# Where the weight casts are issued, and which queue loads the cast weights, in an attention and mixture-of-experts layer on eight cores

## The reference

```
q, k, v = heads(xn @ Wq.T), heads(xn @ Wk.T), heads(xn @ Wv.T)      # 32 heads of 64
z = q @ k.T / 8
lom = where(j < i, -softplus(z), 0);  s = reversed cumsum(lom) - lom
att = where(j < i, exp(log_sigmoid(z) + s), 0)
a = concat(att @ v) @ Wo.T
we = top-4 of softmax(xn @ gate.T), normalized                      # 32 experts
rg, ru = xn @ Rg.T, xn @ Ru.T                                       # 2048 -> 128
y = sum_e we[e] * (((silu(rg @ Ug[e].T @ Cg[e].T) * (ru @ Uu[e].T @ Cu[e].T)) @ Rd.T) @ Ud[e].T @ Cd[e].T)
sh = the same form with a shared expert of width 2816
out = x + a + y + sh
```

## Time and profile before

| | us |
|---|---|
| median of 3 runs | 8175.34 |
| fastest and slowest of them | 8138.22, 8181.30 |
| the profiled execution, its own time | 8143.93 |
| its span on the slowest core | 8142.4 |
| spans of the other cores | 8023.6 to 8126.9 |
| busy in the span: PE, ACT, DVE, POOL | 5775.4, 3040.8, 2680.8, 544.6 |

### The profile page before, as it was taken

How to read it: one execution, slowest core, us unless ns; L and a number is a source line. 1 busy time by engine, 2 the same in 40 slices (tenths; PEclk the granted TensorE clock), 3 DMA queues, 4 the chain that set the end, 5 groups by cost and what they waited for, 6 DMA issues and landing times.

```text
span 8142.4 us, 81258 instructions; the slowest of 8 cores (8023.6 to 8142.4 us)
## 1 busy us (share of the span) xinstructions
PE 5775.4 (71%) x18506; PEld 1757.4 (22%) x18868; DVE 2680.8 (33%) x4660; ACT 3040.8 (37%) x5650; POOL 544.6 (7%) x1028
## 2 busy tenths in 40 slices
PE   2102278888888888889889454777777677777776
PEld 0001122222222222222222121222222222222212
DVE  6300223233233323232232001553255235514550
ACT  0000045555556555556565000443144134403440
POOL 3001111111111111111100000000000000000000
PEclk9996678888789878888895687777877887788878
DMA  9960010000000000000000233212511341153116
GB/s 147 123 73 8 8 12 8 8 8 9 7 8 8 8 8 8 7 8 8 8 3 1 63 85 93 55 49 73 170 49 57 104 124 49 49 153 91 49 33 178
DMA packets 241742, 409.59 MB, mean 50 GB/s; under 512 B 141496, under 2 KB 167752, under 8 KB 235360
## 3 DMA queue, kind: packets, MB, share of 16 engines
q1 hardware_dynamic: 106304, 304.94, 12.2%
q0 software_dynamic: 134976, 99.44, 10.8%
HBM read 452.95 MB, written 85.20 MB: 66 GB/s over the span
## 4 chain that ended last, share of the span: by engine, by line
PE 53%; DMA 16%; DVE 13%; issue 8%; ACT 5%; another core or an unknown queue 3%; DVEq 1%; SPq 0%; ACTq 0%; POOL 0%; POOLq 0%
PE pb L484 10%; PE pb L550 5%; PE pb L529 5%; PE pb L594 5%; DMA cd<-scr_cd 4%; PE pb L754 4%; DVE gu L765 4%; PE pb L589 3%; PE pb L744 3%; DVE lsb L598 3%; PE pb L584 3%; DMA xp<-x 3%; PE pb L867 3%; PE pb L751 3%
## 5 line engine op out<-in xcount | busy, mean ns | idle before, releaser
L598 DVE TENSOR_TENSOR lsb<-lsb,pb 1x512 bf16<-1x512 bf16 (+3 forms) x1152 | 674.2, 585 | 2009.8 <-PE pb L594 1989.3
L572 ACT ACTIVATE texp<-pb 128x512 f32<-128x512 f32 (+3 forms) x1280 | 681.3, 532 | 1226.0 <-PE pb L536 710.0
L765 DVE TENSOR_TENSOR gu<-g,pb 128x512 bf16<-128x512 bf16 x1408 | 957.6, 688 | 394.9 <-PE pb L761 162.0
L757 ACT ACTIVATE g<-pb 128x512 bf16<-128x512 f32 x1408 | 839.6, 597 | 639.6 <-PE pb L751 417.0
L575 ACT ACTIVATE sp<-texp 128x512 bf16<-128x512 f32 (+3 forms) x1280 | 723.7, 565 | 120.5 <-ACT texp L572 4.5
L546 ACT ACTIVATE att<-pb 128x512 bf16<-128x512 f32 (+3 forms) x1280 | 625.8, 523 | 279.5 <-PE pb L589 267.7
L754 PE MATMUL pb<-zu,cgu 128*128 128x512 bf16 x1376 | 587.6, 427 | 143.0 <-DVE gu L765 125.3
L737 ACT ACTIVATE zg<-pb 128x512 bf16<-128x512 f32 x128 | 76.4, 597 | 1519.3 <-PE pb L734 1519.3
L867 PE MATMUL pb<-cd,zd 128*128 128x512 bf16 x2008 | 495.1, 394 | 158.4 <-DMA cd<-scr_cd 114.4
L751 PE MATMUL pb<-zg,cgu 128*128 128x512 bf16 x1374 | 590.5, 430 | 3.3 <-ACT g L757 1.1
L550 PE MATMUL pb<-att,vtok 128*64 128x512 bf16 (+2 forms) x1280 | 535.2, 431 | 59.6 <-ACT att L546 51.1
(11 more groups left out here) (133 smaller groups left out, 4394.7 us busy)
## 6 DMA issues: line engine op xcount, KB each, us to landing
cd<-scr_cd SPq DMA_DIRECT2D x256, 512.0 KB, 4.5
cgu<-scr_cgu SPq DMA_DIRECT2D x136, 704.0 KB, 4.2
scr_cgu<-CguT POOLq DMA_DIRECT2D x32, 704.0 KB, 213.1
x<-x SPq DMA_DIRECT2D x16, 1024.0 KB, 36.9
scr_cd<-CdT POOLq DMA_DIRECT2D x32, 512.0 KB, 216.6
xp<-x SPq DMA_DIRECT2D x64, 256.0 KB, 4.2
out<-op SPq DMA_DIRECT2D x64, 256.0 KB, 2.6
out<-yst POOLq DMA_DIRECT2D x16, 1024.0 KB, 9.4
```

What stands on the lines that cost most here:

```text
L598: Sc.op("DVE", lambda v, lsb=lsb, c0=c0: v.tensor_tensor(lsb[:, c0:QT], lsb[:, c0:QT], pbank[PL][0:1, c0:QT], op=ALU.add), reads=[pr[PL], ...
L757: Sc.op("ACT", lambda sc, c=c, g=g: sc.activation(g[:, c * QT:(c + 1) * QT], pbank[b1][:, 0:QT], AF.Silu), reads=[pr[b1]], writes=[rg_])
L765: Sc.op("DVE", lambda v, c=c, g=g, gu=gu: v.tensor_tensor(gu[:, c * QT:(c + 1) * QT], g[:, c * QT:(c + 1) * QT], pbank[b2][:, 0:QT], op=AL ...
```

## The change

The casts are no longer issued ahead of the layer norm. They are put into a list, the 16 of WoT first and then three for each expert, and in the attention loop one is taken from it at every third step, after that step's pieces. The loads of wo, cgu, u3 and cd move from SP to POOL. werow, xp and the stores of op stay on SP.

```diff
--- before.py
+++ after.py
@@ -268,17 +268,18 @@
         ldc(t_mneg[:, Dd * QT:(Dd + 1) * QT], dr["c_mneg"][Dd * 128:(Dd + 1) * 128, :], "mneg")
     ldc(t_iota[:], dr["c_iota32"], "iota")
 
+    scast_thunks = []
+    for hc in range(NHC):
+        scast_thunks.append(lambda hc=hc: Sc.dma("POOL", "scast", lambda g, hc=hc: g.dma_start(
+            d_wo[hc * 128:(hc + 1) * 128, :], dr["WoT"][hc * 128:(hc + 1) * 128, :]),
+            writes=[res(f"scr_wo{hc}")]))
     for e in range(E):
-        Sc.dma("POOL", "scast", lambda g, e=e: g.dma_start(d_cgu[e * R:(e + 1) * R, :], dr["CguT"][e * R:(e + 1) * R, :]),
-               writes=[res(f"scr_cgu{e}")])
-        Sc.dma("POOL", "scast", lambda g, e=e: g.dma_start(d_cd[e * R:(e + 1) * R, :], dr["CdT"][e * R:(e + 1) * R, :]),
-               writes=[res(f"scr_cd{e}")])
-        Sc.dma("POOL", "scast", lambda g, e=e: g.dma_start(d_u3[e * R:(e + 1) * R, :], dr["U3T"][e * R:(e + 1) * R, :]),
-               writes=[res(f"scr_u3{e}")])
-    for hc in range(NHC):
-        Sc.dma("POOL", "scast", lambda g, hc=hc: g.dma_start(
-            d_wo[hc * 128:(hc + 1) * 128, :], dr["WoT"][hc * 128:(hc + 1) * 128, :]),
-            writes=[res(f"scr_wo{hc}")])
+        scast_thunks.append(lambda e=e: Sc.dma("POOL", "scast", lambda g, e=e: g.dma_start(
+            d_cgu[e * R:(e + 1) * R, :], dr["CguT"][e * R:(e + 1) * R, :]), writes=[res(f"scr_cgu{e}")]))
+        scast_thunks.append(lambda e=e: Sc.dma("POOL", "scast", lambda g, e=e: g.dma_start(
+            d_cd[e * R:(e + 1) * R, :], dr["CdT"][e * R:(e + 1) * R, :]), writes=[res(f"scr_cd{e}")]))
+        scast_thunks.append(lambda e=e: Sc.dma("POOL", "scast", lambda g, e=e: g.dma_start(
+            d_u3[e * R:(e + 1) * R, :], dr["U3T"][e * R:(e + 1) * R, :]), writes=[res(f"scr_u3{e}")]))
 
     s_oF = ExitStack()
     t_oF = sb("oF", [128, NHC * S], BF16, s_oF)
@@ -627,11 +628,15 @@
                     next(nxt)
                 except StopIteration:
                     nxt = None
+            if scast_thunks and step % 3 == 0:
+                scast_thunks.pop(0)()
         while nxt is not None:
             try:
                 next(nxt)
             except StopIteration:
                 nxt = None
+    while scast_thunks:
+        scast_thunks.pop(0)()
 
     close_scope(s2)
     close_scope(s1)
@@ -652,7 +657,7 @@
         t_wo = t_wo2[wsl]
         rwo = res(f"wo{wsl}")
         for hc in range(NHC):
-            Sc.dma("SP", f"lwo{wsl}", lambda s, hc=hc, ft=ft, t_wo=t_wo: s.dma_start(
+            Sc.dma("POOL", f"lwo{wsl}", lambda s, hc=hc, ft=ft, t_wo=t_wo: s.dma_start(
                 t_wo[:, hc * QT:(hc + 1) * QT],
                 d_wo[hc * 128:(hc + 1) * 128, ft * QT:(ft + 1) * QT]),
                 reads=[res(f"scr_wo{hc}")], writes=[rwo])
@@ -713,9 +718,9 @@
 
     def emit_eloads(e, tt):
         cur = e % 4
-        Sc.dma("SP", f"lcgu{cur}", lambda gq, e=e, cur=cur: gq.dma_start(
+        Sc.dma("POOL", f"lcgu{cur}", lambda gq, e=e, cur=cur: gq.dma_start(
             t_cgu[cur][:], d_cgu[e * R:(e + 1) * R, :]), reads=[res(f"scr_cgu{e}")], writes=[res(f"cgu{cur}")])
-        Sc.dma("SP", f"lu3{cur}", lambda gq, e=e, cur=cur: gq.dma_start(
+        Sc.dma("POOL", f"lu3{cur}", lambda gq, e=e, cur=cur: gq.dma_start(
             t_u3[cur][:], d_u3[e * R:(e + 1) * R, :]), reads=[res(f"scr_u3{e}")], writes=[res(f"u3_{cur}")])
         Sc.dma("SP", f"lwer{cur}", lambda s, e=e, cur=cur, tt=tt: s.dma_start(
             t_werow[cur][:], d_we[e:e + 1, tt * QT:(tt + 1) * QT]),
@@ -850,14 +855,14 @@
 
         for half in range(2):
             for ep in range(2):
-                Sc.dma("SP", f"lcd{ep}", lambda g, ep=ep: g.dma_start(
+                Sc.dma("POOL", f"lcd{ep}", lambda g, ep=ep: g.dma_start(
                     t_cd[ep][:], d_cd[ep * R:(ep + 1) * R, :]), reads=[res(f"scr_cd{ep}")], writes=[res(f"cd{ep}")])
             for e in range(E + 1):
                 cur = e % 3
                 rcd = res(f"cd{cur}")
                 if e + 2 < E:
                     nc_ = (e + 2) % 3
-                    Sc.dma("SP", f"lcd{nc_}", lambda g, e=e, nc_=nc_: g.dma_start(
+                    Sc.dma("POOL", f"lcd{nc_}", lambda g, e=e, nc_=nc_: g.dma_start(
                         t_cd[nc_][:], d_cd[(e + 2) * R:(e + 3) * R, :]), reads=[res(f"scr_cd{e + 2}")], writes=[res(f"cd{nc_}")])
                 for tci in range(2):
                     tc = 2 * half + tci
```

## The result

The changed kernel is slower by 0.6%: its median is 8201.61 us (31 runs) against 8155.66 us (31 runs), ratio 1.0058 with a 95% interval of 1.0038 to 1.0078. That is +47 us (31 to 64); the sum of the prediction was +51. The time itself was predicted as 8225 and is 23 us lower: the prediction added its +51 to the median of the first three runs (8175), and the median of 31 is 20 us under that.

The account below looks back on a forecast made before the run. No engine alone bounds the kernel, so TensorE's waits for transfers were priced stage by stage. Terms -250 + 206 - 120 + 74 + 40 + 57 + 44 = +51 us gave 8225 us, range 8115 to 8330.

Parts of the forecast that it names:

- casts out of the start: Start: first rw piece no longer lands behind the casts (-236 us), x tiles land sooner in layer norm (-14); -250 us.
- three waits for wq: Attention: bunched casts on POOL delay wq of head pairs 2 to 4, stalling TensorE 89, 82 and 36 us; +206 us.
- wo on POOL: Output projection: wo for ft 1 to 3 loads beside the ft before, not behind SP's stores; -120 us.
- first expert: Before the first expert: cgu waits on POOL behind rdT and the shared expert's loads; +74 us, bounds 66 and 84.
- cgu behind the stores: Change of token tile: next tile's cgu waits behind the y stores on POOL; +19 us three times, +57 (48 to 70).
- cd: slower load and stores ahead: Down projection: cd stands behind stores between halves (+40 us), and each POOL load takes 0.5 us more (+44).
- The two rivals here: Attention: casts drain faster, small stalls, 8106 us (chance 0.12); or attention itself slows under full DMA engines, 8270 us (0.10).
- The rival that wo gains nothing: Output projection: xp slows as much as wo gets hidden, so the -120 us are gone, 8345 us; chance 0.05.
- the prediction's sign: Start of the experts: first expert matmul of the stage about 105 us after the last output projection.
- The rival that stores and cd cost little: Experts and down projection: loads overtake stores on POOL, cd costs 0.2 us; last three terms about 50, 8135 us; chance 0.13.

Follow-up runs that it names:

- e9: From e6 (only cd on POOL), cd loads of experts 0, 1 and 2 of each half return to SP; ratio 1.0075 to the kernel before, +61 us.
- e1: Casts moved as in the change, all loads left on SP; ratio 0.9970 to the kernel before, -24 us.
- e3: Changed kernel with a cast at every 16th step instead of every third, 7 for each head pair; ratio 0.9828 to the kernel before, -140 us.
- e7: Casts at every 16th step, wo on POOL, cgu, u3 and cd on SP; ratio 0.9583 to the kernel before, -340 us.
- e10: Changed kernel with a cast at every 6th step, 20 for each head pair; attention 3411 us in one profiled execution.
- e11: Changed kernel with a cast at every step, all 112 in head pair 0; attention 3749 us in one profiled execution.
- e4: Kernel before with only the wo loads moved to POOL; ratio 0.9869, -107 us.
- e5: Kernel before with only the cgu and u3 loads moved to POOL; ratio 1.0122, +100 us.
- e6: Kernel before with only the cd loads moved to POOL; ratio 1.0081, +66 us.
- e8: From e7, xp loads issued two blocks ahead, ahead of the store, into four buffers; ratio 0.9431 to the kernel before, -462 us.

## Why the prediction was right, step by step

The measured column takes for each term the mean over all profiled kernels that have the part, less the mean over those that haven't (from the unrounded lengths of the table; e9 is left out for cd).

| term | predicted | measured | shown by |
|---|---|---|---|
| casts out of the start | -250 | -247 | e1, e3, e7 |
| three waits for wq | +206 | +205 (3593 for 3388) | e1; e3, e10, e11 for the cause |
| wo on POOL | -120 | -100 (406 for 506) | e4, e7 |
| first expert | +74 | +77 | e5 |
| cgu behind the stores | +57 | +49 (3 x 16.3) | e5 |
| cd: slower load and stores ahead | +84 | +73 (22 and 51) | e6, e9 in tile 3 |
| sum | +51 | +56 | |

**The start** was right: layer norm's end was put at 289 us and measured at 288.5.

**The waits for wq** were 97, 91 and 31 us on the profiled core for 89, 82 and 36. In the mean of the eight cores the three add to 204, predicted 206. The rate behind them was the weak point named in the prediction, and e10 and e11 bear the account out at bunches of half and of nearly three times the length. The two rivals here fell: the casts did not drain faster, and attention beside them isn't slowed measurably (10 to 26 us with all casts in it in e3, e7 and e8, in a stage that varies by 14 of itself; the small rest wasn't taken apart).

**wo on POOL** is the one term that was mis-sized, by 20 us. The three waits went, as forecast. In the mean over the kernels and cores, the change of ft cost 40.5 us beyond a pitch and not 43.5, a figure from one wait of one core: 9 us less to gain in three. The first wo took 12 us longer, predicted 7. The other 60 pitches grew by 9 us together, predicted 3 (+6), but they add to 321 to 351 us in the kernels with wo on SP alone, so that this last part isn't clear of what varies. The price of sharing, the 6.1 us of xp beside wo for 3.8 without, is that of the slowest core of one execution; all 64 xp loads take 4.3 us in the mean with wo on POOL and 4.2 with it on SP. The rival that wo gains nothing fell with e4.
The rule of the Trainium skill that spoke for that rival (DMA: Bandwidth & Descriptors, Issuing engines are not separate DMA queues) doesn't hold for this kernel as a judgement of size: 100 us are gained by the other queue. Its statement that transfers of all engines interleave on the same DMA engines fits the 6.1 us of xp beside wo.

**First expert, stores, cd.** scd went out 97.0 us after the first rdT load, predicted 89.8 (5125.5 less 5035.7), since the pieces ahead of it came 2.5 to 2.8 us apart and a few up to 4.5, where 2.6 was taken. The first expert matmul came 115 us after the last output projection (4950.50 less 4835.5), where the prediction's sign said about 105 and its own times give 110. The halves' extra is 5.5 us for each first half and 12.7 for each second: so 0.5 us a load, as assumed, and 7 us from the stores (10 predicted). Expert 4 itself starts 10 us later behind the second store, as predicted (22.0 for 11.9 us in the mean of all cores and tiles); the halves win some of it back, more than the prediction allowed. The rival that stores and cd cost little fell with e5 and e6. The first-byte figures of the Trainium skill (DMA: Bandwidth & Descriptors, Latency and other measured facts) would have given an estimate of 0.4 us; the measurement, 0.5, is near.

**The sum** is near for two reasons. No term was far off, and the one error of 20 us was met by errors of 8 and 11 the other way. The second is luck.

## What to carry to other kernels

A transfer without a wait isn't paced by where it stands in a loop: all of them go out as soon as the queue reaches them, and what counts is how long the bunch is against the lead that the queue has over its consumer. With 7 for each pair the same casts cost 10 to 26 us, with 41 some 205.

Moving a load to another queue is to be read as moving it behind other things. wo gained 100 us by leaving the stores of its own stage, cgu lost 126 us and cd 29 by coming to stand behind constants and stores that these loads had no need of, and cd 44 more by loads that are themselves slower on POOL. And a queue that is freed issues its next loads earlier, which can meet what is moving then (e9).

## What was not expected of the hardware

The slowest core of one execution is a poor witness for a few tens of microseconds, since its granted clock differs between executions: the same 300 us stretch of attention on core 4 (columns as in the earlier trace rows) had 830 matmuls at a granted clock of 0.79 before and 914 at 0.93 after, first the kernel before, then the changed one:

```profile
3000.00:3300.00 300.00, 267.61 (x830) 78.24 (x845) 88.27 (x173) 164.15 (x328) 32.18 (x61) 0.79 0.08 7
```
```profile
3000.00:3300.00 300.00, 265.48 (x914) 82.58 (x931) 96.61 (x178) 184.08 (x361) 35.52 (x67) 0.93 0.08 8
```

The stretches don't hold quite the same part of a head pair, but from the q evictions of pair 4 to those of pair 15 the changed kernel was also 37 us faster on this core, after the last wait of the change (from 1754 to 4122 us before, from 1696 to 4027 after). What makes the clock differ there was not tried.
